# Embedding gathers and attention projections in one stage, batch by batch, with q and k of a quad in one product

## What is computed

```
h = base_weight[x]; rows whose id is in tune_ids come from train_weight      # (4, 512, 192)
h = h + attn(layernorm(h))      # 12 heads of 16: q, k, v = products with Wq, Wkv; softmax; Wproj
h = h + switch_ffn(layernorm(h))
h = h + ttt(layernorm(h))       # recurrence over 32 chunks
h = h + soft_experts(layernorm(h))
```

## Time and profile before

| | us |
|---|---|
| median of three runs | 1660.17 |
| the profiled execution, its time and its span | 1645.92, 1644.1 |
| `embed`: start to the block's end | 0 to 56.8 |
| `qkv` | 56.8 to 147.5 |
| `attention` and all after it | 147.5 to 1644.1 |
| PE busy, share of the span | 1335.2, 81% |
| DVE, ACT, POOL busy | 903.3, 769.7, 378.3 |

### The profile page before, as it was taken

One profiled execution on the slowest core, in us unless ns is written; L12 is line 12 of the kernel. 1 busy time (PEld: TensorE's weight loads), 2 busy tenths in 40 slices (PEclk: granted clock), 3 DMA queues, 4 the chain that ended last, 5 costly groups with the idle time before them and its releaser, 6 DMA issues. The chain is left out here.

```text
span 1644.1 us, 29319 instructions
## 1 busy us (share of the span) xinstructions
PE 1335.2 (81%) x10041; PEld 923.9 (56%) x10041; DVE 903.3 (55%) x2160; ACT 769.7 (47%) x1547; POOL 378.3 (23%) x394
## 2 busy tenths in 40 slices
PE   0363999969947999489999994889885888799989
PEld 0131233334634777367777773677764334399989
DVE  2230988841246777268778783987874676400001
ACT  0231355632113444179879792575753333343433
POOL 6324000000005777434344341000000232200000
PEclk9976799976878999789999997999986999999999
DMA  1025122100012333423333334221205000089951
GB/s 47 25 58 94 34 56 59 40 22 0 1 45 70 116 117 117 134 75 100 112 113 97 105 99 120 64 68 34 54 1 136 9 0 1 0 217 288 299 146 38
DMA packets 113819, 132.03 MB, mean 80 GB/s; under 512 B 28015, under 2 KB 99614, under 8 KB 113608
## 3 DMA queue, kind: packets, MB, share of 16 engines
q1 hardware_dynamic: 112168, 128.86, 28.1%
q0 software_dynamic: 1536, 1.59, 0.4%
HBM read 91.62 MB, written 37.09 MB: 78 GB/s over the span
## 5 line engine op out<-in xcount | busy, mean ns | idle before, releaser
L572 DVE TENSOR_REDUCE mx<-bank 128x1 f32<-128x512 f32 x192 | 119.7, 682 | 40.6 <-PE bank L494 40.2
L632 ACT ACTIVATE PT<-bank 128x1024 f32<-128x1024 f32 x96 | 94.5, 1024 | 85.3 <-PE bank L510 84.7
L2192 POOL TENSOR_TENSOR m_cw<-m_E,m_f 128x1024 f32<-128x1024 f32 x16 | 45.1, 2818 | 376.7 <-DVE m_f L2137 376.7
L1563 POOL TENSOR_SCALAR r_grD<-gr 32x192 f32<-32x192 f32 x128 | 68.7, 536 | 170.6 <-DVE gr L1466 141.1
L1345 PE MATMUL bank<-r_grD,ek 128*128 128x256 f32 x384 | 104.9, 411 | 0.0
L2277 DVE TENSOR_TENSOR x_eo<-bank,b 128x192 f32<-128x192 f32 x32 | 11.5, 358 | 154.7 <-PE bank L2254 154.7
L2243 PE MATMUL bank<-slT,w 96*128 x768 | 92.7, 279 | 3.2 <-ACTq L45 2.0
L2265 ACT ACTIVATE x_g<-bank,w 128x128 f32<-128x128 f32 x192 | 53.2, 376 | 87.8 <-PE bank L2243 87.8
L494 PE MATMUL bank<-K,Q 97*128 97x512 bf16 x192 | 70.1, 419 | 29.6 <-POOL K L647 26.5
L2243 PEld LDWEIGHTS bank<-slT,w 96*128 96x128 f32 x768 | 90.4, 195 | 5.4 <-issue 4.8
L1345 PEld LDWEIGHTS bank<-r_grD,ek 128*128 128x128 f32 x384 | 70.7, 198 | 13.8 <-ACT r_std L1486 0.5
(11 more groups left out here) (330 smaller groups left out, 3225.1 us busy)
## 6 DMA issues: line engine op xcount, KB each, us to landing
w<-in_m_w SPq DMA_DIRECT2D x32, 579.0 KB, 6.7
w<-in_m_w SPq DMA_DIRECT2D x32, 576.0 KB, 6.3
ek<-k_d SPq DMA_DIRECT2D x34, 384.0 KB
k_d<-p_krows SPq DMA_DIRECT2D x48, 256.0 KB, 2.5
tgt<-c_d SPq DMA_DIRECT2D x34, 196.0 KB
c_d<-p_rows SPq DMA_DIRECT2D x32, 196.0 KB, 2.8
g_d<-gr SPq DMA_DIRECT2D x32, 192.0 KB
o_G<-g_d SPq DMA_DIRECT2D x32, 192.0 KB, 3.0
```

Of the source, the lines that this page charges most:

```text
L572: v.tensor_reduce(mx[u % 2][:, j // 4, j % 4:j % 4 + 1], slot(f"A{u}.{j}"), AX.X, ALU.max).then_inc(*dve.did(f"max{u}.{j}"))
L632: a.activation(PT[kt % 2][:, 2 * hp:2 * hp + 2, :], STB[s % 2][:, :, :], ACT.Exp, scale=DH ** -0.5)\
L1563: last = g_.tensor_scalar(grD[g][rr, :, b, :], b3(gr[j % RING][rr, cols(g)]), 0.0, None, ALU.bypass)
```

## The change

`qkv` is gone, and `embed` does its work in the same block. `V1` and `qk_d` are made ahead of it.

- Gathers: POOL issues the base gathers of batches 0, 1 and 2, the train gathers of 0 and 1, the base gathers of 3, the train gathers of 2 and 3. Train gathers of a batch wait for the base gathers of that batch, and each batch has its own semaphore on which DVE's layer norm waits.
- Order: the loop is written out. DVE's layer norm of batch b+1 and ACT's square root of it stand ahead of the splitting of batch b, and ACT's `xT` copies of b+1 ahead of the `mid` copies of b. `parts` has two copies, used in turn.
- Products: the weights `a_wqk` are laid out on the host so that for each quad 64 rows of q and 64 of k stand side by side. Three products of 128 output rows take the place of four of 96. The split is 3 x 128x512 per part and batch, where it was 4 x 96x512. SP issues 24 stores of 64 rows where it was 32 of 32 or 64.
- `lo` moves from POOL to DVE.
- The memsets of `V1` on POOL move ahead of the gathers; the load of `ident` moves ahead of that of the tune ids, and the turn of the ids waits for `ident` alone, not for three constants.

```diff
+        wqk, wv = sb("a_wqk", [DC, KC, QUADS, P]), sb("a_wv", [DC, KC, D])
+        parts, rest = [sb(f"a_parts{r}", [P, QUADS, SPLIT, N], BF16) for r in range(2)], sb("a_rest", [P, QUADS, N])
...
+                sp.dma_start(M["ident"][:, :], ins["c_ident"]).then_inc(known, 16)
                 sp.dma_start(tune_i[:, :], ins["tune_ids"].rearrange("(a n) -> a n", a=1).to_broadcast([P, NT]))\
                     .then_inc(loaded, 16)
-                sp.dma_start(M["ident"][:, :], ins["c_ident"]).then_inc(consts, 16)
+                sp.dma_start(wqk[:, :, :, :], ins["a_wqk"].rearrange("(k p) c n -> p k c n", p=DC)).then_inc(weights, 16)
+                sp.dma_start(wv[:, :, :], ins["WvT"].rearrange("(k p) n -> p k n", p=DC)).then_inc(weights, 16)
...
+                    for c in C:
+                        sp.wait_ge(*dve.at(f"lo{c}.{b}"))
+                        for w in range(2):
+                            sp.dma_start(qk_d[b, c, w].rearrange("s r n -> r s n"),
+                                         parts[b % 2][w * E1:(w + 1) * E1, c, :, :]).then_inc(stored[b % 2], 16)
...
+                t_.wait_ge(known, 16)
+                t_.wait_ge(*dve.at("idsf"))
+                t_.transpose(IDS[:, 0:TILES], ids16f[:, :], ident[0:TILES, 0:TILES]).then_inc(turned, 1)
+                t_.wait_ge(weights, 32)
+                for b in SB:
+                    t_.wait_ge(*dve.at(f"xn.{b}"))
+                    if b:
+                        t_.wait_ge(*act.at(f"xT1.{b - 1}"))
+                    for k in range(KC):
+                        for t in range(TB):
+                            last = t_.transpose(T[k][0:DC, t * P:(t + 1) * P], xn[:, t, k * DC:(k + 1) * DC], ident[:, :])
+                        last.then_inc(*pe.did(f"T{k}.{b}"))
+                    t_.wait_ge(*act.at(f"xT1.{b}"))
+                    for c in C:
+                        if b:
+                            t_.wait_ge(*dve.at(f"rest{c}.{b - 1}"))
+                        for k in range(KC):
+                            last = t_.matmul(QK[c], wqk[:, k, c, :], xT[:, k, :], start=(k == 0), stop=(k == 1))
+                        last.then_inc(*pe.did(f"qk{c}.{b}"))
+                    for j in range(2):
+                        if b:
+                            t_.wait_ge(*act.at(f"v{j}.{b - 1}"))
+                        for t in (2 * j, 2 * j + 1):
+                            for k in range(KC):
+                                last = t_.matmul(VB[j][:, (t % 2) * D:(t % 2 + 1) * D], xT[:, k, t * P:(t + 1) * P], wv[:, k, :],
+                                                 start=(k == 0), stop=(k == 1))
+                        last.then_inc(*pe.did(f"v{j}.{b}"))
...
+                def layer_norm(b):
+                    v.wait_ge(laid[b], 16 * TB)
...
+                layer_norm(0)
+                for b in SB:
+                    if b + 1 < B:
+                        layer_norm(b + 1)
+                    for c in C:
+                        v.wait_ge(*act.at(f"hi{c}.{b}"))
+                        if b:
+                            v.wait_ge(*dve.at(f"lo{c}.{b - 1}"))
+                        v.tensor_tensor(rest[:, c, :], QK[c], parts[b % 2][:, c, 0, :], ALU.subtract).then_inc(*dve.did(f"rest{c}.{b}"))
+                    for c in C:
+                        v.wait_ge(*act.at(f"mid{c}.{b}"))
+                        v.tensor_tensor(parts[b % 2][:, c, 2, :], rest[:, c, :], parts[b % 2][:, c, 1, :], ALU.subtract)\
+                            .then_inc(*dve.did(f"lo{c}.{b}"))
...
+                root(0)
+                turned_rows(0)
+                for b in SB:
+                    if b + 1 < B:
+                        root(b + 1)
+                    for c in C:
+                        a.wait_ge(*pe.at(f"qk{c}.{b}"))
+                        if b >= 2:
+                            a.wait_ge(stored[b % 2], 16 * 2 * QUADS * (b // 2))
+                        a.activation(parts[b % 2][:, c, 0, :], QK[c], ACT.Copy).then_inc(*act.did(f"hi{c}.{b}"))
+                    for j in range(2):
+                        a.wait_ge(*pe.at(f"v{j}.{b}"))
+                        a.wait_ge(ones, 2)
+                        a.activation(V1[:, b * TB + 2 * j:b * TB + 2 * j + 2, :, 0:DH],
+                                     VB[j][:, 0:2 * D].rearrange("p (t h d) -> p t h d", t=2, h=HA), ACT.Copy)\
+                            .then_inc(*act.did(f"v{j}.{b}"))
+                    if b + 1 < B:
+                        turned_rows(b + 1)
+                    for c in C:
+                        a.wait_ge(*dve.at(f"rest{c}.{b}"))
+                        a.activation(parts[b % 2][:, c, 1, :], rest[:, c, :], ACT.Copy).then_inc(*act.did(f"mid{c}.{b}"))
...
+                g.memset(V1[:, :, :, DH:DH + 1], 1.0).then_inc(ones, 1)
+                g.memset(V1[:, :, :, DH + 1:VP], 0.0).then_inc(ones, 1)
                 g.wait_ge(*dve.at("ids"))
-                for t in range(TILES):
-                    g.indirect_dma_start(out=h[:, t, :], out_offset=None, in_=ins["base_weight"],
-                                         in_offset=bass.IndirectOffsetOnAxis(ap=ids_u[:, t:t + 1], axis=0))\
-                        .then_inc(gathered, 16)
-                g.wait_ge(gathered, 16 * TILES)
-                g.wait_ge(*dve.at("tuned"))
...
+                def train(b):
+                    g.wait_ge(based[b], 16 * TB)
...
+                base(0)
+                base(1)
+                base(2)
+                train(0)
+                train(1)
+                base(3)
+                train(2)
+                train(3)
+                for b in SB:
+                    g.wait_ge(laid[b], 16 * TB)
...
-def qkv(nc, M, ins):
...
-        embed(nc, M, ins)
         with ExitStack() as c1:
             M["V1"] = c1.enter_context(nc.sbuf_tensor("V1", [P, TILES, HA, VP], F32))
             M["qk_d"] = nc.dram_tensor("qk_d", (B, QUADS, 2, SPLIT, 4 * DH, N), BF16, kind="Internal").ap()
-            qkv(nc, M, ins)
+            embed(nc, M, ins)
...
-        "WqT": g["L0_attn_Wq"].T, "WkT": kv[:, 0].reshape(D, D).T, "WvT": kv[:, 1].reshape(D, D).T,
+        "WvT": kv[:, 1].reshape(D, D).T,
+        "a_wqk": np.stack([g["L0_attn_Wq"].T.reshape(D, QUADS, 4 * DH), kv[:, 0].reshape(D, D).T.reshape(D, QUADS, 4 * DH)], 2)
+        .reshape(D, QUADS, P),
```

More of the change, by code:

```diff
@@ L125, in _ @@
                     .then_inc(*dve.did("tuned"))
+                v.memset(eps[:, :], LN_EPS).then_inc(*dve.did("eps"))
+                def layer_norm(b):
+                    v.wait_ge(laid[b], 16 * TB)
+                    for t in range(TB):
+                        last = v.bn_stats(stats[:, t, :], h[:, b * TB + t, :])
+                    last.then_inc(*dve.did(f"stats.{b}"))
+                    v.wait_ge(*dve.at(f"stats.{b}"))
+                    v.memset(gate[:, :], 0.0)
+                    if b:
+                        v.wait_ge(*act.at(f"std.{b - 1}"))
+                    for t in range(TB):
+                        last = v.bn_aggr(mv[:, t, :], stats[:, t, :])
+                    last.then_inc(*dve.did(f"aggr.{b}"))
+                    v.wait_ge(*act.at(f"std.{b}"))
+                    v.reciprocal(rstd[:, :], std[:, :]).then_inc(*dve.did(f"rstd.{b}"))
+                    v.wait_ge(*dve.at(f"rstd.{b}"))
+                    if b:
+                        v.wait_ge(*pe.at(f"T1.{b - 1}"))
+                    for t in range(TB):
+                        last = v.tensor_scalar(xn[:, t, :], h[:, b * TB + t, :], mv[:, t, 0:1], rstd[:, t:t + 1], ALU.subtract, ALU.mult)
+                    last.then_inc(*dve.did(f"xn.{b}"))
@@ new lines, in _, with root, turned_rows @@
+            @block.scalar
+            def _(a):
+                act.open(a)
+                a.wait_ge(*dve.at("eps"))
+                def root(b):
+                    a.wait_ge(*dve.at(f"aggr.{b}"))
+                    if b:
+                        a.wait_ge(*dve.at(f"rstd.{b - 1}"))
+                    a.activation(std[:, :], mv[:, :, 1], ACT.Sqrt, bias=eps[:, 0:1]).then_inc(*act.did(f"std.{b}"))
+                def turned_rows(b):
+                    for k in range(KC):
+                        a.wait_ge(*pe.at(f"T{k}.{b}"))
+                        a.activation(xT[:, k, :], T[k][0:DC, :], ACT.Copy).then_inc(*act.did(f"xT{k}.{b}"))
+                root(0)
[19 more added lines that the diff above has]
+                        a.activation(parts[b % 2][:, c, 1, :], rest[:, c, :], ACT.Copy).then_inc(*act.did(f"mid{c}.{b}"))
@@ L173, in ln_std, with base @@
[L173 to L185 removed]
+                def base(b):
+                    for t in range(b * TB, (b + 1) * TB):
+                        g.indirect_dma_start(out=h[:, t, :], out_offset=None, in_=ins["base_weight"],
+                                             in_offset=bass.IndirectOffsetOnAxis(ap=ids_u[:, t:t + 1], axis=0)).then_inc(based[b], 16)
```

175 lines of the change are left out of this document (33 added, 142 removed).

## The result

The changed kernel takes 1598.0 us, the median of four runs (1590.0 to 1609.5), where the kernel before takes 1656.58 (1652.84 to 1668.04, four runs). The ratio is 0.967, with a 95% interval of 0.962 to 0.972. On another chip the same pair gave 0.9645 (0.960 to 0.969). The profiled execution of the changed kernel took 1609.5 us, its span is 1607.7. Ratios leave out an execution more than 1.5% above the fastest of its kernel, which was one, of the kernel with mask rows and loads ahead.

What follows compares the result with a forecast made beforehand. Bound by POOL's gather list, then a chain of waits. Rows 32.1, batch 0 16.7, rounds 32.1 and tail 7.5 put attention at 88.4 us instead of 147.5: gain 59.1, from 1660.2 to 1601, range 1590 to 1618.

Steps and rivals of the forecast that it cites:

- First batch's rows: Gathers before the first layer norm: only twelve base and four train gathers stand ahead, so rows are there at 32.1 us.
- Batch 0: First batch from statistics through turns and three products to v: 16.7 us, PE through at 48.8.
- Rounds: Batches 1 to 3, paced by PE: 10.7 us each, 32.1 in all, ending at 80.9.
- Tail: From the last v to attention: copy, three mid, last lo, stores and block end, 7.5 us; attention starts at 88.4.
- the clock falls between batches: Rival: PE's clock drops before the products of batches 1 to 3, costing 6.5 us, total 1608; chance 0.13.
- DVE and POOL get in each other's way: Rival: gathers beside DVE's work are held by 3.5 us, gain 24, total 1636; chance 0.07 shared with clock never up.
- Slower: Rival: stages from 500 us on get a lower clock; 0.873 instead of 0.94 makes the result 1% slower; chance 0.01.
- signs of being wrong: Forecast is wrong if attention starts after 98 us, or the stretch behind it differs from 1497 by over 8 us.
- later stages that take or give over 10 us: Case after attention's start: chance 0.04, of which 0.03 ends within 1% and 0.01 slower.

Runs made afterwards that it cites:

- kernel with mask rows and loads ahead: Early square-root table, tune ids loaded second, plus POOL writing attention's mask rows and SP loading two quads in the first block: 0.957 of the kernel before.
- kernel with all rows first: Changed kernel with all sixteen base gathers ahead of the train gathers and the first layer norm waiting for all 32: attention opens at 110.34 us, not 87.95.
- kernel with the early table: Changed kernel with tune ids loaded second again and a spare square root on ACT as soon as eps is set: attention opens at 86.20 us, not 87.95.
- more turns: Changed kernel with PE making each run of turns three times, 24 a batch instead of 8: attention opens at 92.8 us, not 87.95.
- more pause: Changed kernel with ACT copying the second half of the turned rows four more times before the copy PE awaits: attention opens at 99.37 us, not 87.95.
- norm behind the split: Changed kernel with the next batch's layer norm, square root and xT copies behind this batch's splitting: attention opens at 120.2 us, 0.980 of the kernel before.

## Why the prediction was right

The forecast was 1601 us, gain 59; the median is 1598.0, and by medians the gain is 58.6. The 3 us between the two times are the starting point: 1601 was taken from 1660.2, and with a fourth run the median of before is 1656.58. By its own steps:

1. *First batch's rows*, 32.1 forecast, 31.76 measured, by two errors that cancel. The ids came 1.04 us later (first gather at 6.74, has 5.70), which I had put at nothing. And the rows landed 1.2 us after the fourth train gather's issue, where I had taken 2.55 from a wait behind 16. That only the first four train gathers lie on the path is seen in the timeline after, where the layer norm starts at 31.76 and twelve more are issued behind it or beside it; the kernel with all rows first shows what waiting for them costs.

2. *Batch 0*, 16.7 forecast, 18.6 measured (31.76 to 50.37). Statistics to turns took 4.87 instead of 3.70. The table load of 1.28 us waits for the same signal as the square root behind it, and stands bare at 33.40 (above); before, it started at 56.98, beside the statistics (the earlier trace rows begin with them at 57.23). The kernel with the early table shows it. The rest is the products, which took 8.4 us instead of 7.5; with the same lists up to there they took 7.3 to 8.8 in the other profiles, with more or fewer of the passes at 0.86 us.

3. *Rounds*, 10.7 forecast, 9.62 measured, 3.2 us better in three. The mis-sized term is the turns: at the high clock they take 1.04 us, not 2.0; the lower bound of 1.1 was right. The rest of the term held: 12 passes at 0.43, v 2.76, 0.73 of pause.

4. *Tail*, 7.5 forecast, 8.7 measured. The last `lo` ends 3.0 us behind v, as worked out; from there to attention's opening it takes 5.7 us, not 4.5. SP issues the last six stores from 81.04 to 85.0, 2.8 us past the last `lo`, and landing and block end follow. That fewer stores would help is not seen here.

The sum is right to 0.5 us because +1.9 and +1.2 meet -0.3 and -3.2. That the sizes cancel is luck. The mechanism is not: each step of the sum was there, in its order. The parts, each by its own kernel: gathers (order and overlap) 22.4 us, order 32.2, merged product 7.4, `lo` 0.7. Undone one at a time they add up to 62.7, 3 us more than the 59.6; the changed kernel also pays for what was bared (table load, ids, tail), and parts undone singly need not add up.

Of the rivals, *the clock falls between batches* did not come. Its case did not arise as it was priced: turns took 1.04 us and not 2.0, so even without counting them the pause was 1.8 us and not 2.8. The kernels with more turns and with more pause go further, and speak against the reason given for it: turns hold the clock, and can raise it. *DVE and POOL get in each other's way* did not come with gathers: `xn` took 1.25 and 1.30 us beside them, gathers 0.96 beside `xn`. It came with memsets (6.93 us). The Trainium skill, page "SBUF — State Buffer" ("Who interferes with whom"), has POOL locked out of its port by a two-port DVE instruction, and the loser of either kind waiting for the other. The trace agrees in kind for memsets beside `xn` (6.93 us), and does not show it for gathers beside `xn` (1.25 and 1.30 us).

*Slower* did not come: by the medians, less the 1.8 us between time and span, the stretch from attention's opening to the end takes 1507.2 us before and 1508.3 after. But one of the prediction's own signs of being wrong did come. It says that this stretch must not differ from 1497 by over 8 us, and in the profiled execution it takes 1519.8. The kernel before, profiled again, has 1516.2. So the sign was set too narrowly, from a single execution of before, and the span of 1585.0 that was forecast on top of it was missed (1607.7). The chance of 0.04 for later stages that take or give over 10 us was too small for one execution.

The experts' stage spreads by 24 us over the profiles (145.9 to 170.1). The medians of a few runs agree with the forecast all the same; one profile does not.

## What to carry to other kernels

In a list that an engine runs in order, ask which instruction of the next batch stands behind which of this one: 32 of 60 us here came from moving the next batch's layer norm, with its square root and copies, ahead of this one's splitting. When work is moved beside other work, look for what was free only because something else was late: a table load, a landing, the tail's issue queue. Compare two kernels at the point where the edited part ends, and not only by their spans, when a later stage varies by more than the step that is being judged.

## What the runs showed of the hardware

- Runs of f32 transposes count as work for TensorE's clock, by the durations: after 24 of them (4.78 us, the later ones at the fast rate) the products began at the fast rate, after 8 (1.92 us) seven or eight of twelve still went at the slow rate (8.4 us for 12).
- Behind 2.7 us without work of PE the clock fell in two of three batches, about 1 us into the next products; behind 1.8 us, of which 1.0 were turns, in no round of the eight profiles that have such rounds. In longer pauses it fell 1.9 us after PE's last pass (norm behind the split, batch 0), 2.9 us (before) and 3.9 us (changed kernel, last batch): the length of a pause alone doesn't tell.
- The profile's PEclk reads 1.00 through batch 0 of the changed kernel, while its first seven passes take 0.86 us, as they do where it reads 0.50.
- Four `tensor_scalar` of 128x192 took 1.25 us alone, 1.25 to 1.44 beside gathers, 2.77 beside POOL's `tensor_tensor`, 6.93 beside POOL's memsets of one to three partitions (1.80 to 1.92 us each).
- The third gather takes 4.43 or 4.44 us in every profile, wherever the first starts (5.69 to 6.99), and always ends 0.8 us behind the run of sixteen lookups on DVE. What ties the two was not tried.
- The same experts' stage moved 228 to 266 GB/s over the profiles, and took 170.1 to 145.9 us. Two profiles of one kernel, the one before, have 266 and 239 GB/s.
